# Gating of a four-layer graph and mixture kernel rebuilt: column halves, centred router tokens, logits by tile

## The reference

```python
x = x + _L0_gnn_ref(_layernorm(x), edge_index, ...)        # h = x@W+b; out = relu(sum_i w_i * adj^i @ h), 3 steps
x = x + _L0_ffn_ref(_layernorm(x)[None], ...)[0]           # 8 experts, 512 -> 1024 -> 512, gelu, top 2
x = x + _L1_gnn_ref(_layernorm(x), edge_index, edge_attr)  # messages over 4352 edges, then a GRU update
x = x + _L1_ffn_ref(_layernorm(x)[None], ...)[0]           # router, 8 LSTM experts, top 2
```

```python
# gating of layer 2 (first mixture)
logits = relu(xf @ gw1 + gb1) @ gw2 + gb2; top 2 of 8; softmax of the two
# end of layer 3 (graph layer): gi = agg @ W_ih.T + b_ih; gh = h @ W_hh.T + b_hh
r = sigmoid(i_r + h_r); z = sigmoid(i_z + h_z)
n = tanh(i_n + r * h_n)
h_new = (1.0 - z) * n + z * h
return h + gamma * (h_new - run_mean) * rsqrt(run_var + eps) + beta
# gating of layer 4 (LSTM mixture)
logits = flat_x @ router_w + router_b; top 2 of 8; softmax of the two
# its experts' step, from state 0: c = sigmoid(i) * tanh(g); h = sigmoid(o) * tanh(c); y = h @ Wo + bo
```

## Time and profile before

| | us |
|---|---|
| median of 3 runs | 464.31 |
| lowest, highest | 463.85, 465.33 |
| the profiled execution | 466.27 |
| its span (first to last instruction) | 464.5 |
| mean granted clock of TensorE | 0.972 |
| TensorE busy | 433.6 |
| VectorE busy | 390.9 |
| ScalarE busy | 296.0 |
| GpSimd busy | 111.0 |

### The profile page before, as it was taken

How to read it: one execution, slowest core, us unless ns; L and a number is a source line. 1 busy time by engine, 2 the same in 40 slices (tenths; PEclk the granted TensorE clock), 3 DMA queues, 4 the chain that set the end, 5 groups by cost and what they waited for, 6 DMA issues and landing times.

```text
span 464.5 us, 6169 instructions
## 1 busy us (share of the span) xinstructions
PE 433.6 (93%) x2206; PEld 348.3 (75%) x2206; DVE 390.9 (84%) x629; ACT 296.0 (64%) x343; POOL 111.0 (24%) x128
## 2 busy tenths in 40 slices
PE   4999999999999995798999999999999999999994
PEld 2655778888888775676899998668788787886773
DVE  6978799888889776598999996868999988878775
ACT  7966368778877761724444455437788887849741
POOL 3842000111100023167877200122003121000300
PEclk9999999999999998799999999967999999999999
DMA  7941568999998855987767233235789999975901
GB/s 236 327 147 45 182 234 313 323 344 369 365 375 320 322 189 181 377 326 226 208 206 252 78 131 142 90 141 198 281 315 354 379 356 353 381 283 190 397 22 49
DMA packets 25942, 116.20 MB, mean 250 GB/s; under 512 B 7069, under 2 KB 7741, under 8 KB 15025
## 3 DMA queue, kind: packets, MB, share of 16 engines
q1 hardware_dynamic: 18544, 93.91, 54.6%
q0 software_dynamic: 7216, 21.79, 14.5%
q10 hardware_dynamic: 144, 0.02, 0.0%
HBM read 109.15 MB, written 6.55 MB: 249 GB/s over the span
## 4 chain that ended last, share of the span: by engine, by line
PE 64%; DVE 15%; DMA 11%; ACT 4%; issue 3%; SPq 1%; POOL 1%; DVEq 0%; ACTq 0%; POOLq 0%
PE bank L1584 11%; PE bank L1585 11%; PE bank L1589 11%; DMA xg<-node_rows,idx 4%; DVE wlo L981 4%; PE bank L1575 3%; PE bank L1576 3%; PE bank L1577 3%; PE bank L1983 3%; PE bank L1981 3%; PE bank L1598 2%; PE bank L1868 2%; PE bank L1803 2%; DMA gath<-node_rows,src_i 1%; DMA raw<-in_weights_dram 1%
## 5 line engine op out<-in xcount | busy, mean ns | idle before, releaser
L981 DVE TENSOR_TENSOR wlo<-raw,whi 128x2048 fp32r<-128x2048 f32 x72 | 163.2, 2287 | 20.0 <-ACT whi L687 19.5
L687 ACT ACTIVATE whi<-raw 128x2048 fp32r<-128x2048 f32 x73 | 138.0, 1914 | 15.5 <-PE bank L1950 8.5
L1584 PE MATMUL bank<-whi,xe_hi 128*128 128x512 f32 x192 | 78.3, 408 | 1.5 <-ACT xe_hi L723 0.7
L1585 PE MATMUL bank<-wlo,xe_hi 128*128 128x512 f32 x192 | 76.8, 400 | 0.0
L630 POOL DMA_INDIRECT xg<-node_rows,idx x14 | 19.5, 1392 | 148.2 <-DVE idx L1258 139.5
L1589 PE MATMUL bank<-whi,xe_lo 128*128 128x512 f32 x192 | 53.2, 399 | 0.0
L1584 PE MATMUL bank<-whi,hT_hi 128*128 128x512 f32 (+1 forms) x124 | 47.1, 387 | 2.8 <-ACT hT_hi L746 1.8
L663 POOL DMA_INDIRECT gath<-node_rows,src_i x34 | 42.4, 1247 | 15.3 <-DVE mp L1505 6.7
L1585 PE MATMUL bank<-wlo,hT_hi 128*128 128x512 f32 (+1 forms) x124 | 45.4, 373 | 0.0
L1584 PEld LDWEIGHTS bank<-whi,xe_hi 128*128 128x128 f32 x192 | 36.7, 191 | 10.0 <-issue 1.4
L1589 PEld LDWEIGHTS bank<-whi,xe_lo 128*128 128x128 f32 x192 | 36.6, 191 | 9.1 <-DVE xe_lo L1251 0.3
(11 more groups left out here) (312 smaller groups left out, 872.7 us busy)
## 6 DMA issues: line engine op xcount, KB each, us to landing
raw<-in_weights_dram SPq DMA_DIRECT2D x85, 1024.0 KB, 6.7
y_rows<-y_sb POOLq DMA_DIRECT2D x16, 256.0 KB, 6.8
ea<-in_ea_dram SPq DMA_DIRECT2D x8, 256.0 KB
node_rows<-xn POOLq DMA_DIRECT2D x4, 256.0 KB, 2.5
gath<-node_rows,src_i POOLq DMA_INDIRECT x34
x<-in_x_dram SPq DMA_DIRECT2D x1, 512.0 KB, 3.8
gw<-in_L_ffn_gw_dram SPq DMA_DIRECT2D x1, 512.0 KB, 8.7
node_rows<-A_sb POOLq DMA_DIRECT2D x2, 256.0 KB, 5.1
```

What stands on the lines that cost most here:

```text
L687: act.activation(whi[n % SPL][:, :, :], raw[n % RAW][:, :, :], ACT.Copy).then_inc(hi_cut, 1)
L981: dve.tensor_tensor(wlo[n % SPL][:, :, :], raw[n % RAW][:, :, :], whi[n % SPL][:, :, :].bitcast(f32), ALU.subtract).then_inc(lo_cut, 1)
L1584: pe.matmul(ps, xh[:, blocks + k, :], whi[w % SPL][:, k, cs], start=first and k == 0, stop=False)
L1585: pe.matmul(ps, xh[:, blocks + k, :], wlo[w % SPL][:, k, cs], start=False, stop=False)
```

## The change

It has three places.

First gating: the drain is gone; the selectors move from the gating to the graph layer's last idle time; tile 0 is normalised before tile 1's statistics; TensorE's 24 fillers become 15, and 6 stand between the two tiles' transposes; the logits of the tiles go to two banks; the cast of the indices is gone (the one-hot compares with the integer); the positions are signalled after three of the five matmuls; `over` comes after the first G.

Begin of the second graph layer: token sums, last add and moments go tile by tile; tile 0's xn comes between tile 1's two sums; tile 1's transposes stand inside tile 0's first product; the low part of each tile waits for that tile's high part alone; SyncE's loads of edge attributes wait for the copy of tile 1 (xt_sb) instead of the drain.

End of the second graph layer and LSTM gating: tile 1's last Wih product, candidate, tanh, blend, add and statistics go in halves of 256 columns; the product of (1 - z) with the scale g2s moves from VectorE to GpSimd; the router's tokens are centred, not scaled, so that they need no rstd; the logits are made from them and scaled by rstd when the bias is added; ScalarE scales xn afterwards and makes its high part, tile by tile; each logits matmul repeats the router's 8 columns 8 times (COPIES), so it is 64 wide; fillers of 5, 14, 2, 5 and 2 become 3, 3, 3, 3, 6 and 3; VectorE's cut of LSTM chunk 1 moves from the gating to behind xe_first, and ScalarE's cut of chunk 3 too.

```diff
-            sp.wait_ge(layer_done, 2)
+            sp.wait_ge(xt_sb, 2 * NT + 2)
...
-            root(3)
+            for n in range(NT):
+                pool.wait_ge(g1["u"], n + 1)
+                pool.tensor_tensor(gh[:, n, 1, :], rz[:, n, 1, :], g2s[:, :], ALU.mult).then_inc(g1["gh_sb"], 1)
+                root(3, (n,))
...
             def gating(nth):
-                xT_copy(2 * nth - 1, xnT, None if nth == 1 else first + 2 * SPL + 3)
-                cut_to(SPL if nth == 1 else CHUNK[LSTM_ORDER[0]] + SPL)
-                act.wait_ge(xn_ok, NT * (2 * nth - 1) + NT)
-                act.activation(xn_hi[:, :, :], xn[:, :, :], ACT.Copy).then_inc(gate["xn_cut"], 1)
+                for n in range(NT):
+                    xT_copy(2 * nth - 1, n, xnT)
+                    if nth == 2:
+                        act.wait_ge(rstd_ok, 3 * NT + n + 1)
+                        act.activation(xn_hi[:, n, :], xn[:, n, :], ACT.Copy, scale=rstd[:, n:n + 1])\
+                           .then_inc(gate["xn_cut"], 1)
+                        act.wait_ge(gate["xn_cut"], 2 * n + 2)
+                        act.activation(xn[:, n, :], xn[:, n, :], ACT.Copy, scale=rstd[:, n:n + 1])\
+                           .then_inc(gate["xn_cut"], 1)
...
+            def centre(n):
+                dve.tensor_scalar(xn[:, n, :], x[:, n, :], mv[:, n, 0:1], None, ALU.subtract).then_inc(xn_ok, 1)
...
+                    else:
+                        dve.wait_ge(rstd_ok, 3 * NT + n + 1)
+                        link(dve.scalar_tensor_tensor(out=lg[:, n, :], in0=B[6 + n][:, 0:E], scalar=rstd[:, n:n + 1],
+                                                      in1=gb[:, 1, :], op0=ALU.mult, op1=ALU.add))
...
                 for n in range(NT):
+                    if run.layer == 0:
+                        for k in range(2):
+                            link(token_sum(n, k))
+                            if n == 1 and k == 0:
+                                normalise(2, (0,))
...
-                dve.tensor_tensor(gh[:, n, 1, :], rz[:, n, 1, :], g2s[:, :], ALU.mult)
                 link(dve.tensor_tensor(x[:, n, :], x[:, n, :], gh[:, n, 0, :], ALU.subtract))
...
+            candidate(1, B[3][:, 0:D // 2], HALVES[0])
+            dve.wait_ge(chunk_used, CHUNK[("gnn", "Wih", 2)] + 1)
+            candidate(1, B[7][:, 0:D // 2], HALVES[1])
+            blend(1, 0, HALVES[0])
+            tokens(1, HALVES[0])
+            blend(1, 1, HALVES[1])
+            spread(1, 0, HALVES[0])
+            tokens(1, HALVES[1])
+            spread(1, 1, HALVES[1])
+            moments(1, 2)
...
+            def lstm_logits(n):
+                pe.wait_ge(xt_sb, 3 * NT + n + 1)
+                for k in range(KB):
+                    ins = pe.matmul(B[6 + n][:, 0:COPIES * E].rearrange("p (r e) -> p r e", r=COPIES),
+                                    xnT[:, n, k, :], rw[:, k, :].unsqueeze(1).to_broadcast([P, COPIES, E]),
+                                    start=k == 0, stop=k == KB - 1)
                 ins.then_inc(gate["lg_ps"], 1)
...
+            def lstm_gating():
+                turn_x(3, (0,))
+                keep_busy(B[0], 3)
+                lstm_logits(0)
+                keep_busy(B[0], 3)
+                turn_x(3, (1,))
+                keep_busy(B[0], 3)
+                lstm_logits(1)
+                keep_busy(B[0], 6)
+                positions(2)
...
-            keep_busy(B[0], 5)
+            keep_busy(B[0], 3)
             pe.wait_ge(g1["u"], NT)
-            turn_x(3, (0,))
-            keep_busy(B[0], 14)
-            pe.wait_ge(layer_done, 3)
-            gating(2)
+            lstm_gating()
             experts(lstm)
```

More of the change, by code:

```diff
@@ L62 @@
 SUMS = 2
+POS = 128
+COPIES = 8
 MSG = 3
@@ L546, in _, with root @@
                       allow_small_or_imprecise_dtypes=True).then_inc(iota_ok, 1)
-            def root(layer):
-                for n in range(NT):
+            def root(layer, tiles=range(NT)):
+                for n in tiles:
                     pool.wait_ge(var_ok, NT * layer + n + 1)
@@ L701, in cut_to, with xT_copy @@
                     done[0] += 1
-            def xT_copy(layer, dst, cut):
-                for n in range(NT):
-                    if n and cut:
-                        cut_to(cut)
-                    act.wait_ge(xt_ps, NT * layer + n + 1)
-                    act.activation(dst[:, n, :, :], quarters(B[5 - n]), ACT.Copy).then_inc(xt_sb, 1)
+            def xT_copy(layer, n, dst):
+                act.wait_ge(xt_ps, NT * layer + n + 1)
+                act.activation(dst[:, n, :, :], quarters(B[5 - n]), ACT.Copy).then_inc(xt_sb, 1)
             def experts(run):
@@ L771, in more_cuts @@
                         more_hi(run, q)
+                cuts(run.base + SPL - run.layer)
+                xe_first()
                 cuts(run.base + SPL)
-                xe_first()
                 act.wait_ge(gate["d"], run.layer + 1)
@@ L1274, in token_sums @@
                             if k:
[L1275 to L1278 removed]
+                                dve.wait_ge(sum_ok, n + 1)
+                            token_sum(n, k).then_inc(sum_ok, 1)
                 def outputs(e):
@@ L1347, in experts @@
                 build_g(0)
+                overflow(run.layer + 1)
                 build_g(1)
@@ L1395, in before @@
                     else:
-                        token_sums()
+                        if run.layer:
+                            token_sums()
                         next_layer()
@@ L1549, in tokens @@
-            def tokens(n):
-                dve.wait_ge(g1["n"], n + 1)
-                link(dve.tensor_tensor(rz[:, n, 2, :], rz[:, n, 2, :], gh[:, n, 1, :], ALU.mult))
-                link(dve.tensor_tensor(x[:, n, :], x[:, n, :], rz[:, n, 2, :], ALU.add))
-            for n in range(NT):
-                reset(n)
-                if n == 1:
-                    cut_half(first + 2 * SPL, 1)
-                update(n)
-                candidate(n)
-                if n == 0:
-                    cut_half(first + 2 * SPL, 0)
-                else:
-                    normalise(3, (0,))
-                tokens(n)
-                moments(n)
@@ L1566, in _, with candidate, blend, tokens @@
-            dve.drain().then_inc(layer_done, 1)
+            def candidate(n, ps, cs):
+                dve.tensor_tensor(rz[:, n, 2, cs], rz[:, n, 0, cs], ps, ALU.add).then_inc(g1["n_in"], 1)
+            def blend(n, h, cs):
+                dve.wait_ge(g1["n"], n + h + 1)
+                dve.wait_ge(g1["gh_sb"], NT + n + 1)
+                link(dve.tensor_tensor(rz[:, n, 2, cs], rz[:, n, 2, cs], gh[:, n, 1, cs], ALU.mult))
+            def tokens(n, cs):
+                link(dve.tensor_tensor(x[:, n, cs], x[:, n, cs], rz[:, n, 2, cs], ALU.add))
@@ new lines, in _ @@
+            reset(0)
+            update(0)
+            dve.wait_ge(g1["gi_ps"], 3)
+            candidate(0, B[2][:, :], slice(0, D))
+            cut_half(first + 2 * SPL, 0)
+            blend(0, 0, slice(0, D))
+            tokens(0, slice(0, D))
+            spread(0)
+            moments(0)
+            reset(1)
+            cut_half(first + 2 * SPL, 1)
+            centre(0)
+            update(1)
+            dve.wait_ge(g1["gi_ps"], 4)
+            candidate(1, B[3][:, 0:D // 2], HALVES[0])
@@ L1577, in mm3, with product @@
                 return pe.matmul(ps, xl, wh, start=False, stop=last, skip_group_check=skip)
-            def product(ps, xh, xl, w, blocks, lo_ready, first, last, cs=slice(0, C), half_ready=None):
+            def product(ps, xh, xl, w, blocks, lo_ready, first, last, cs=slice(0, C), half_ready=None, between=None):
                 for k in range(KB):
@@ L1689, in _, with positions @@
                 ins.then_inc(g0["u_ps"], 1)
-            def gating(nth):
-                turn_x(2 * nth - 1, range(NT) if nth == 1 else (1,))
+            def positions(nth):
+                pe.wait_ge(gate["mask"], nth)
+                ps, counts = B[6][:, POS:POS + 2 * E], B[7][:, POS:POS + E]
+                pe.matmul(ps[:, 0:E], tri[:, 0:P], mask[:, 0, :], start=True, stop=True)
+                pe.matmul(ps[:, E:2 * E], tri[:, P:T], mask[:, 0, :], start=True, stop=False)
+                pe.matmul(ps[:, E:2 * E], tri[:, 0:P], mask[:, 1, :], start=False, stop=True)\
+                  .then_inc(gate["pos_ps"], 1)
+                pe.matmul(counts, tri[:, P:T], mask[:, 0, :], start=True, stop=False)
+                pe.matmul(counts, tri[:, P:T], mask[:, 1, :], start=False, stop=True).then_inc(gate["pos_ps"], 1)
```

210 lines of the change are left out of this document (112 added, 98 removed).

## The result

| | before | changed |
|---|---|---|
| median, us | 464.08 (4 runs) | 469.36 (468.06 to 469.8, 4 runs) |
| profiled execution, us (span) | 466.27 (464.5) | 469.05 (467.3) |
| mean granted clock | 0.972 | 0.980 |

The ratio of changed to before is 1.0094 (95% interval 1.0059 to 1.0128): slower, by 0.94%. I had forecast 460.9 us, with 8% for slower, and for another reason than the one that made it so. In the two profiled executions the mean granted clock is even higher than before.

A forecast was written before the change was run, and what follows sets the result against it. It took chains of dependent steps off TensorE and half clock at the router to bound the changed places, TensorE the steady LSTM layer. C -3.7, A -0.35, B +0.65 gave -3.4: 464.31 to 460.9 us, range 458.6 to 463.4.

The forecast's parts named there:

- 8% for slower: First gating: the clock falls to 0.50 at the wide product and costs +5.4 us, giving 466.3; chance 0.08.
- Part A: First gating, normalised and turned tile by tile: -0.35 us, bounds -0.6 and +0.1.
- Part B: Begin of the second graph layer, tile by tile, with two close A_sb writes: +0.65 us, bounds -0.5 and +2.6.
- Graph layer's begin costs 2.6 instead of 0.65: Rival at the second graph layer's begin: close writes and late loads cost 2.6 us, giving 462.8; chance 0.12.
- Part C: End of the second graph layer, LSTM gating and LSTM start, the largest part: -3.7 us.
- step 1: Last Wih product to router tokens, in halves of 256 columns: -1.55 us, with +0.15 for TensorE's cost.
- Step 6: Product moved to GpSimd, beside VectorE's update of tile 1: +0.4 us, bounds 0 and +1.3.
- Steps 2 to 4: Second gating: tokens to mask -1.5 us, mask to gather -0.6, gather and first product at full clock -1.9.
- Step 5: LSTM start: VectorE's cut of chunk 1 behind xe_first adds 2.28 us; the idle of 1.08 takes in 1.0.
- clock rival for each gating: Clock falls again in the second gating: 462.7 us, chance 0.15; in the first gating: 466.3, chance 0.08.

The follow-up runs named there:

- e1: Changed kernel with SyncE's edge loads and the weight chunks behind them waiting for VectorE's variance of tile 1 instead of ScalarE's copy; ratio to before 1.0032.
- e2: Changed kernel with the product with g2s back on VectorE instead of GpSimd; ratio to before 1.0102.
- e9: Changed kernel with the old begin of the second graph layer, the g2s product on VectorE and more_experts behind step 3; median 460.43 us, ratio to before 0.9873.
- e7: Changed kernel with the router's logits 8 columns wide instead of 64 (COPIES = 1); ratio to before 1.0065.
- e4: Changed kernel with 13 filler matmuls in TensorE's pause before expert 1 in the LSTM layer; ratio to before 1.0041.
- e12: e9 with more_experts put back ahead of step 0 of the LSTM layer; ratio to before 0.9955.
- e8: Changed kernel with the whole begin of the second graph layer as before, SyncE waiting for tile 1's variance; ratio to before 0.9989.
- e11: e9 with the product with g2s put back on GpSimd; ratio to before 0.9916.
- e5: Kernel before with SyncE's edge loads and weight chunks waiting for ScalarE's copy of tile 1 instead of the drain; ratio to before 1.0007.
- e10: e9 with SyncE waiting for ScalarE's copy of tile 1 again; ratio to before 0.9929.
- e3: Changed kernel with more_experts of the LSTM layer moved from ahead of step 0 to behind it; ratio to before 1.0051.

## Why the prediction was wrong

**Part A: right.** -0.35 forecast, -0.3 measured, clock 1.00 at the wide product.

**Part B: the step that failed most.** It is the term for the write of A_sb. I had +0.65 (to +2.6), from "two writes of 256 KB that share the queues could cost half of one's 5.17 more". Measured +3.9 at the first mp. The rival "Graph layer's begin costs 2.6 instead of 0.65" named the place and the late loads, with 12% and too low a price. I had counted what the moved wait holds back as the edge loads alone (0.75 MB). Behind them in SyncE's queue stand four weight chunks of 1 MB, and in the earlier trace rows the write's 5.17 us is that of a write with the first two chunks 9.3 and 3.9 us ahead of it; now they leave 3.1 and 1.5 us ahead of it, and the write takes 8.97. e1 gives 2.9 us back with that line alone; the closeness of the two writes, which my sum was about, cost little (5.53 in e1, which has it too).

**Part C, step 1:** -1.55 forecast, -1.4 with what the halves cost TensorE. From the end of the last Wih matmul to the centred tile 5.26 us became 5.02 in the changed kernel, and 4.37 in e2 and e9, which have no product on GpSimd. So step 1 by itself gave -0.9. The size that was off: the halves follow each other at 0.46 us, not at 0.38 (each takes the 0.42 of the earlier trace rows at 312.61, and there is a gap behind it), which is 0.5 over seven. **Step 6** I had priced at +0.4 within 0 and +1.3; it cost 0.65 (5.02 against 4.37), by holding the centring of tile 0, not the update of tile 1. The Trainium skill's "SBUF — State Buffer", section "Who interferes with whom", states that the later of the two is blocked for the whole instruction, which would be the 1.29 us of GpSimd here; measured were 1.0 to 1.1 us, and e2 takes them away, so the trace agrees but for some 0.2 us. I had weighed that rule and still taken the value from a 128x1 operation, the nearest row in kind but not in length.

**Steps 2 to 4: right.** Tokens to mask -1.8 (forecast -1.5), mask to gather -0.7 (-0.6), gather to first product -1.8 (-1.9). The granted clock held at both, here and in all the profiles with this gating. The reason that I gave was not shown (e7), so that they came out may in part be luck.

**Step 5: the mechanism was half seen.** I let the weight cut cost 2.28 and have "the idle of 1.08" take 1.0 of it in. In fact VectorE went from idle to late: the activation product comes 1.06 us later, TensorE 3.1 us too early, and the pause costs it the clock. I also had the path wrong. I took the weight cut for what expert 1's second chunk waits for, but the one recorded wait of TensorE there was at the first chunk, for the gathered tokens, which come behind VectorE's activation product and ScalarE. TensorE's timeline of before:

```profile
327.03 0.50 PE L1584 MATMUL bank<-whi,xe_hi 128*128 128x512 f32 x1 [0.74 <-ACT xe_hi L723]
```

That a faster gating opens a pause, and the pause a slow stretch, was in none of my cases: I had a clock rival for each gating and none for what comes behind. e4 puts the clock at 2.4 us (its interval overlaps the changed kernel's) and e12 the whole pause at 3.8 (clear of e9's).

**The sum.** -3.4 forecast, +2.8 between the profiles: 6.2 us apart. By the table of events: part B 3.9 instead of 0.65 (3.3), steps 1 and 6 -0.2 instead of -1.0 (0.8), steps 2 to 4 -4.3 instead of -4.0 (-0.3), step 5 +3.3 instead of +1.3 (2.0), and 0.45 behind expert 1, which I had at nothing. The medians are a further 2.5 us apart, which this account does not explain. The runs bear out the first and the fourth in the total time (clearly in e8 and e12, with just overlapping intervals in e1 and e4), the second only in the rows of the trace (e2, e11).

## What to carry to other kernels

A wait that is moved on a queue moves everything queued behind it: list these transfers with their bytes and ask which urgent small transfer they now fall beside. When one stage gets faster, look at which engine arrives early at the next join; its pause costs twice if the clock falls in it, and a few fillers there, or moving non-urgent small operations to where their engine has slack, give it back. Work moved from VectorE to GpSimd isn't free for VectorE: here each GpSimd instruction of 1.29 us put 1.0 to 1.1 us on the VectorE operation that ran beside it.

## What I had not expected of the hardware

- The last write of 256 KB took at most 5.9 us where the queue's loads had left earlier (5.17 before, 5.53 in e1, 5.88 in e12), and 8.0 to 9.3 us where they left just ahead of it (the changed kernel, e2 to e5, e7, e10), with no order by the DMA share beside it.
- A 128x512 product takes 1.29 us on GpSimd and 0.69 on VectorE. A VectorE operation with one tile and a column of scalars as input (the centring, 0.48) was held as long as one with two tiles (0.69): 1.53 and 1.82.
- The granted clock of one place is not a fixed property of a program's order there: the second gating of the same instructions had 1.00 in the profiles of the changed kernel, e1 and e3, and 0.50 in 308 to 310 in e4's, whose edit comes later.
